# Graph-attention kernel: q and k taken from the fp16 halves of m, cosines of unnormalised m with the threshold subtracted in PSUM, and cross-partition maxima by TensorE

## The reference, cut to what matters

```python
# layer 0: 8 heads of 64, h = relu(layernorm(x)), 128 x 128 x 512
m   = h @ map_w.T + map_b
n   = m_head / max(norm(m_head), 1e-8)
adj = (n @ n.T > 0.1)                       # cosine threshold, per head
q   = m @ q_w.T + q_b ;  k = m @ k_w.T + k_b
p   = softmax(mask(q @ k.T / 8)) * keep
a   = adj * p
v   = h @ gcn_map_w.T + gcn_map_b
x   = x + relu((a @ v) @ gcn_W.T / (a.sum(-1) + 1))
# layer 1: 4 heads of 64, plain masked attention
h1  = relu(layernorm(x));  x = x + attention(h1 @ Wq, h1 @ Wk, h1 @ Wv, mask) @ Wo + bo
```

## Time and profile before

| what | value |
|---|---|
| median of 3 runs | 2621.02 us (2617.14 to 2621.39) |
| profiled execution | 2623.38 us, its span 2621.6 us |
| mean granted TensorE clock | 0.989 of full speed |
| PE busy | 2554.7 us, 97% of the span |
| PEld busy | 2056.4 us, 78% |
| POOL busy | 2164.7 us, 83% |
| DVE busy | 2068.1 us, 79% |
| ACT busy | 1709.5 us, 65% |
| DMA | 299 MB moved, engines busy 61% of the time in the steady part |

### The profile page before, as it was taken

How to read it: one execution, slowest core, us unless ns; L and a number is a source line. 1 busy time by engine, 2 the same in 40 slices (tenths; PEclk the granted TensorE clock), 3 DMA queues, 4 the chain that set the end, 5 groups by cost and what they waited for, 6 DMA issues and landing times.

```text
span 2621.6 us, 78827 instructions
## 1 busy us (share of the span) xinstructions
PE 2554.7 (97%) x30681; PEld 2056.4 (78%) x30681; DVE 2068.1 (79%) x3467; ACT 1709.5 (65%) x4509; POOL 2164.7 (83%) x2450
## 2 busy tenths in 40 slices
PE   6899999999999999999999999999999999999995
PEld 4678878887887887887887887887888888788784
DVE  6478788788888888788878888888888888888875
ACT  3366676676676676676676667667667667667664
POOL 2388888888888888888888888888888888888874
PEclk8999999999999999999999999999999999999998
DMA  5145665665665665665665666566566556556554
GB/s 134 45 83 115 121 119 112 121 123 108 118 129 102 118 129 103 120 125 113 115 125 111 117 121 117 111 125 117 112 121 124 113 113 129 112 112 129 109 95 97
DMA packets 830707, 299.08 MB, mean 114 GB/s; under 512 B 772608, under 2 KB 780288, under 8 KB 830336
## 3 DMA queue, kind: packets, MB, share of 16 engines
q1 hardware_dynamic: 830336, 294.04, 57.9%
HBM read 75.80 MB, written 33.55 MB: 42 GB/s over the span
## 4 chain that ended last, share of the span: by engine, by line
PE 90%; DVE 3%; POOL 2%; issue 2%; DMA 2%; ACT 1%; SPq 0%; DVEq 0%; ACTq 0%; POOLq 0%
PE unit_ps L1563 49%; PE unit_ps L1571 24%; PE s_ps L1581 4%; PE s_ps L1623 3%; PE c_ps L1581 3%; PE unit_ps L1642 2%; PE unit_ps L1657 2%; PE unit_ps L1581 2%; PE unit_ps L1633 1%; DMA o_t<-o_hl 1%; DVE qk_hl L1131 1%; POOL inv_norm L700 1%; ACT e_ec L828 0%; ACT qk_hl L918 0%; PE c_ps L1520 0%
## 5 line engine op out<-in xcount | busy, mean ns | idle before, releaser
L828 ACT ACTIVATE e_ec<-e_ec,neg_mx 128x128 f32<-128x128 f32 x1016 | 392.9, 388 | 4.1
L1563 PE MATMUL unit_ps<-h_t,w_m_hi 128*128 128x256 f16 x2048 | 343.1, 275 | 12.6 <-DMA h_t<-h_hl 12.6
L1563 PE MATMUL unit_ps<-h_t,w_q_hi 128*128 128x256 f16 x2048 | 345.0, 274 | 2.6 <-DVE bias_q L1382 2.6
L1563 PE MATMUL unit_ps<-h_t,w_k_hi 128*128 128x256 f16 x2048 | 345.3, 274 | 0.1
L1571 PE MATMUL unit_ps<-w_v_hi,h_t 128*128 128x512 f16 x1024 | 324.9, 379 | 0.0
L651 POOL TENSOR_TENSOR e_ec<-e_ec 128x1024 f16<-128x1024 f32 x126 | 285.9, 2269 | 12.1 <-ACT e_ec L856 12.1
L1563 PE MATMUL unit_ps<-h_t,w_m_lo 128*128 128x256 f16 x1024 | 280.8, 274 | 0.0
L1563 PE MATMUL unit_ps<-h_t,w_k_lo 128*128 128x256 f16 x1024 | 280.5, 274 | 0.0
L1563 PE MATMUL unit_ps<-h_t,w_q_lo 128*128 128x256 f16 x1024 | 280.1, 274 | 0.0
L1131 DVE TENSOR_TENSOR qk_hl<-qk_sb,qk_hl 128x512 f16<-128x512 f32 x128 | 173.2, 1353 | 121.0 <-ACT qk_hl L918 121.0
L1563 PEld LDWEIGHTS unit_ps<-h_t,w_m_hi 128*128 128x128 f16 x2048 | 196.4, 98 | 42.4 <-issue 13.1
(11 more groups left out here) (207 smaller groups left out, 7736.7 us busy)
## 6 DMA issues: line engine op xcount, KB each, us to landing
xa<-in_x_dram SPq DMA_DIRECT2D x128, 256.0 KB, 3.7
xres<-in_x_dram SPq DMA_DIRECT2D x128, 256.0 KB, 2.8
out_dram<-ybuf SPq DMA_DIRECT2D x128, 256.0 KB, 2.5
h_t<-h_hl SPq DMA_TRANSPOSE x256, 3.2
ec_t<-e_ec SPq DMA_TRANSPOSE x254, 3.2
adj_in<-in_adj_dram SPq DMA_DIRECT2D x128, 16.0 KB, 2.0
p_t<-p_hl SPq DMA_TRANSPOSE x128, 3.3
o_t<-o_hl SPq DMA_TRANSPOSE x128, 3.7
```

Source lines behind the costliest of these rows:

```text
L828: ins = nc.scalar.activation(e[:, h, :], e[:, h, :], ACT.Exp, bias=neg[:, h:h + 1], scale=SCALE, accum_out=sums[:, h:h + 1])
L1563: ins = nc.tensor.matmul(out, w[a][:, i, c * P:(c + 1) * P], h[:, :, b, i, :], start=n == 0, stop=n == len(passes) - 1)
```

## The change

q and k are now made from `m`: its two fp16 halves (`m_hl`, double buffered, made by ScalarE `m_upper` and GpSimd `m_lower` in the even slot, right after `m`) are the moving operand of `q` and `k`, and the weights `q_w` and `k_w` are only turned and split. The same halves are both operands of the cosines, without any division: into the same PSUM bank TensorE adds a product that is -0.1 \* |m_i| \* |m_j| (`norm_t`, `norm_r`), and `gate` compares with 0. The norms (power +1/2) are cut into fp16 parts by GpSimd, turned by two small matmuls (unit `nt`), and VectorE's `threshold_rows` writes them out as `norm_t` (128x128) and `norm_r` (128x1024, times a mask of -1). Maxima over partitions come from a transpose, a VectorE maximum and a small matmul; for six weights the sum of squares takes the place of the maximum. SP loads `x` first. `m_upper` stands in ScalarE's even slot between `e_upper` and the second `l1_exp`. In the prologue `make` and `bias` go, for q and for k. The split of layer 1's weights moves from the prologue into slots 0 and 1. One of the two `result_base` goes from the even to the odd slot.

```diff
 UNITS = (
     (("s1a", -4), ("s1b", -4), ("m01", 2), ("m23", 2), ("wo", -5), ("va", 2), ("lv", -4), ("vb", 3)),
-    (("q01", 1), ("o1e", -5), ("q23", 1), ("o1o", -4), ("norm", 1), ("k01", 1), ("lq", -3), ("bc0", 1), ("bc1", 1), ("k23", 1),
+    (("q01", 1), ("o1e", -5), ("q23", 1), ("o1o", -4), ("norm", 1), ("k01", 1), ("lq", -3), ("k23", 1), ("nt", 1), ("unused", B_MAX),
      ("lk", -3), ("wo", -5)),
 )
...
+            load_x(Slot(-5, None, B))
             load_columns(st_map, map_w, map_in)
-            load_x(Slot(-5, None, B))
-            load_weights()
-            for n in (-3, -2, -1):
+            load_first_weights()
+            first = Slot(-3, None, B)
+            turn_x(first)
+            load_adj(first)
+            load_x(first)
+            load_other_weights()
+            for n in (-2, -1):
...
-            def inverse_norms(s):
+            def norm_rows(s):
-                    nc.gpsimd.tensor_tensor(inv_norm[:, :], sq_sum[:, :], minus_half[:, :], ALU.pow).then_inc(inv_norm_done, 1)
+                    nc.gpsimd.tensor_tensor(norm[:, :], sq_sum[:, :], plus_half[:, :], ALU.pow).then_inc(norm_done, 1)
...
+                    nc.gpsimd.tensor_copy(parts[:, :, 1:4, :], rows.unsqueeze(2).broadcast_to([P, 2, 3, 2 * C])).then_inc(norm_split, 1)
+                    nc.gpsimd.tensor_tensor(parts[:, :, 0:5:4, :], rows.unsqueeze(2).broadcast_to([P, 2, 2, 2 * C]),
...
-            def directions_lower(s, g):
-                    nc.gpsimd.tensor_tensor(dir_hl[:, 1, :, cols], m_sb[:, :, cols], dir_hl[:, 0, :, cols],
-                                            ALU.subtract).then_inc(dir_lo, 1)
+            def m_lower(s):
+                if s.has(2):
+                    b = (s.n + 2) // 2 % 2
+                    pool.wait_ge(m_hi, s.at(lambda t: (t + 2) // 2 + 1))
+                    nc.gpsimd.tensor_tensor(m_hl[:, b, 1], m_sb[:, :, :], m_hl[:, b, 0], ALU.subtract).then_inc(m_lo, 1)
...
+            def m_upper(s):
+                    nc.scalar.activation(m_hl[:, b, 0], m_sb[:, :, :], ACT.Copy).then_inc(m_hi, 1)
...
-            def directions(s, g):
+            def threshold_rows(s):
+                    nc.vector.tensor_copy(norm_t[:, :], unit_ps[:, u.bank, 0:P])
+                    nc.vector.tensor_tensor(norm_r[:, :, :, :].rearrange("p g c n -> p (g c) n"),
...
             def cosines(s):
-                    row_pairs([[c_ps[:, a, c * P:(c + 1) * P] for c in range(C)] for a in range(2)], dir_hl, dir_hl,
-                              columns(s.n % 2)).then_inc(c_full, 1)
+                    row_pairs([[c_ps[:, a, c * P:(c + 1) * P] for c in range(C)] for a in range(2)], parts, parts,
+                              columns(s.n % 2), last=False)
+                    u = s.unit("nt", back=1 + s.n % 2)
+                    pe.wait_ge(unit_out[u.bank], u.before + 1)
+                    for a in range(2):
+                        r = slice(a * DK, (a + 1) * DK)
+                        ins = nc.tensor.matmul(c_ps[:, a, :], norm_t[r, :], norm_r[r, s.n % 2].rearrange("p c n -> p (c n)"),
+                                               start=False, stop=True)
...
-            make("make_q", "turn_q")
-            bias("bias_q")
-            evicted("make_q")
+            evicted("turn_q")
             qk_part(before_0, "q", w_q, 0)
```

More of the change, by code:

```diff
@@ L41 @@
 UNROLL = 8
[L45 to L48, removed]
+NAMED = 14
+MAP, MAP_B, GM, QW, KW, L_FIRST = 0, 4, 5, 8, 9, 10
+M, M_OUT, V, V_OUT, Q, K, LQ, LK, WO, LV, LV_OUT = range(11)
+SCALED = 11
 BLOCKED = 1e30
@@ L421, in build @@
-        ONES = 4
-        def prep_at(kind, part=0):
-            u = PREP.index((kind, part))
-            place = u - C
-            if place < 0:
-                return unit_ps[:, part], None, 0, u + 1
-            bank = (s_ps[:, place % 4].rearrange("p b n -> p (b n)") if place % 4 < 2 else c_ps[:, place % 4 - 2])
-            return bank, prep_out[place % PREP_BANKS], place // PREP_BANKS, u + 1
+                (p1_sb[:, :, :, :].rearrange("p b h n -> p (b h n)").rearrange("p (c n) -> p c n", c=C), Wv, w_lv, LV)]
@@ new lines, in build @@
+        ONES = 14
+        def prep_at(kind, part=0):
+            full = PREP.index((kind, part)) + 1
+            if kind == "turn_m":
+                return unit_ps[:, part], None, 0, full
+            if kind in SMALL:
+                return s_ps[:, 0].rearrange("p b n -> p (b n)"), prep_out[0], SMALL.index(kind), full
+            place = STAGED.index(kind) * C + part
+            bank = (s_ps[:, 1].rearrange("p b n -> p (b n)"), c_ps[:, 0], c_ps[:, 1])[place % 3]
+            return bank, prep_out[1 + place % 3], place // 3, full
@@ L1581, in row_pairs @@
                             ins = nc.tensor.matmul(outs[half][c], st[r, a, c, cols], mv[r, b, c, cols],
-                                                   start=n == 0, stop=n == 2)
+                                                   start=n == 0 and (last or c == 0), stop=last and n == 2)
                 return ins
@@ L1673, in qk_part @@
                 if s.has(1):
-                    features(s, f"{name}{2 * half}{2 * half + 1}", w, 2 * half, h_t[:, (s.n + 1) // 2 % 2])
+                    pe.wait_ge(m_lo, s.at(lambda t: (t + 1) // 2 + 1))
+                    ps = start_unit(s, f"{name}{2 * half}{2 * half + 1}")
+                    parts = m_hl[:, (s.n + 1) // 2 % 2]
+                    for c in (2 * half, 2 * half + 1):
+                        passes = [(i, a, b) for b in range(2) for i in range(C) for a in range(2 - b)]
+                        for n, (i, a, b) in enumerate(passes):
+                            ins = nc.tensor.matmul(ps[:, c % 2 * 2 * P:(c % 2 + 1) * 2 * P], w[a][:, i, c * P:(c + 1) * P],
+                                                   parts[:, b, i, :], start=n == 0, stop=n == len(passes) - 1)
+                    ins.then_inc(unit_full, 1)
             def v_part(s, name, a):
```

500 lines of the change are left out of this document (280 added, 220 removed).

## The result

The changed kernel takes 2659.55 us (median of 4 runs, 2658.73 to 2663.12), the kernel before on the same chip 2621.2 (2617.14 to 2626.93). The ratio is 1.0147 with a 95% interval of 1.0126 to 1.0169: slower by 38 us, where 2662 was forecast.

A forecast was written before the change was run, and what follows sets the result against it. PE was taken to bound the steady part, with a new wait at lk after the change. 2623.4 - 36 (prologue) + 77 (pairs) = 2664, or 2662 us for the median; range 2635 to 2700 (58%), 8 in 10 within 2560 to 2715.

The forecast's parts named there:

- The prologue's term: Before slot 0: -38.6 us, plus 2.6 for layer 1's weights in slots 0 and 1, sum -36; slot 0 near 64.
- the pairs': Steady part: a pair of 40.2 us against 38.92, +1.28 each, +77 us for 60 pairs.
- The bound before: Steady part before the change: as long as PE's work, busy 2313.55 of 2320 us, with POOL next.
- PE's own sum: PE's work in a steady pair: -0.87 + 0.11 + 0.43 = -0.33 us, so 38.45 if PE stays the bound.
- The place and the mechanism: Before lk in the odd slot: later x_lower and k_lower held by POOL's e_lower make PE wait 1.75 us.
- The second of the two ways: Start of lk by POOL's queue order: e_lower ends 17.0 to 17.7 us into the odd slot, lk at 18.2 to 18.9.
- the one late pair of before: Trace pair with x_lower 5.71 us into the odd slot and lk at 18.78; model for the 18.7 taken.
- the 1.10 us of room: Before lk: lqk_lower frees the bank at about 363.57, PE comes at 364.67; this room hid POOL's work.
- rival A: Steady part: the chain to lk keeps off PE, a pair is 38.45 us, the kernel 2557 to 2570; chance 20%.
- The cause of the late landing: POOL's even slot: m_lower, 2.13 us behind e_lower, delays x_lower and behind it SP's o_hl transpose.
- 0.15 us taken: VectorE's odd slot: threshold_rows stands ahead of the next mask and adds 0.15 us to a pair's chain, between 0 and 0.65.
- rival D: Steady part: PE's clock falls in the new pause, costing up to 240 us, or 20 to 60; 13% shared with another rival.

The follow-up runs named there:

- e12: e10 with GpSimd's two small operations of keep_and_block moved, in odd slots, from ahead of x_lower to just ahead of e_lower; 2563.17 us.
- e3: The changed kernel without the 128x1024 instruction of threshold_rows from slot 0 on; 2656.39 us.
- e4: The changed kernel with m_lower on VectorE, behind x1_stats of the even slot, in place of GpSimd; 2651.79 us.
- e5: The changed kernel with SP's transposing DMA of o_hl issued ahead of the two loads of x in the odd slot; 2581.45 us.
- e8: The changed kernel with four moves in the prologue's order on ScalarE and VectorE, steady part as it is; 2647.23 us.
- e9: The changed kernel without GpSimd's m_lower from slot 1 on; 2630.79 us.
- e10: The changed kernel with the moves of e5 and e8 together; 2573.38 us.
- e1: The kernel before with one more GpSimd subtraction of 128x1024 behind e_lower in each even slot, its result unread; 2736.98 us.

## Why the prediction was right, and where it was not

The sum of the changes by stage, from the two traces: until slot 6, 190.88 - 213.55 = -22.7 us; the 59 pairs to slot 124, (2541.17 - 190.88) - (2510.01 - 213.55) = +53.8; the end, 117.1 against 111.6, +5.5. Together +36.7, the difference of the spans (2658.3 - 2621.6). The prediction had -36 and +77. The prologue's term was too large by 13 us, the pairs' by 23, the end (+5.5) was not in it; the errors cancelled, and that 2662 is so near to 2659.55 is luck; the parts don't deserve it.

The bound before, and PE's own sum: right. 38.45 for PE's pair was met to the hundredth in the won pairs and in e12. The two 512-column cosine matmuls cost 0.22 a slot (17.50 against 17.28).

The place and the mechanism: right in what was seen, too coarse in what decides. `lk` waits in 55 of 59 pairs, for `lqk_lower` behind `k_lower`, which the lock holds until POOL's `e_lower` is over. The second of the two ways (by POOL's order) gave `e_lower`'s end as 17.0 to 17.7 and `lk` as 18.2 to 18.9; measured 17.00 and 18.35. `x_lower` began 5.59 us into the odd slot, not 6.0 to 6.5, which is why `e_lower`'s end is at the near end. I took 18.7, from the one late pair of before, and these 0.35 us are the whole error of the forecast pair (40.2 against 39.87 in a usual one). The direct reading of the queue was better than the nearest disturbed pair, which had its own delay.

What I did not see is that this is a race and not a sum. Seven kernels have the changed steady part with `e_lower` mostly at 14.87 us into the slot (the changed one, e3, e4, e5, e8, e9, e10); they have 413 pairs from slot 6 to slot 124. In 129 `k_lower` starts 0.01 us or more ahead of `e_lower`: each is won and takes 38.45 us (two at slot 6 take 38.65 and 38.68). The other 284 are late, at 39.84 us or more; in two of them the records have `k_lower` ahead by less than 0.01. Where `e_lower` starts later the border moves with it. In the kernel before (mostly 15.22) and in e1 (mostly 16.05 or 16.37), 118 more pairs, all with a lead of 0.04 us or more are won and all others wait at `lk`; so it is the order that decides and not a time in the slot. The page "SBUF — State Buffer" of the Trainium skill (section "SBUF: two separate sides") says that whichever of the two operations starts first has the shared ports for its whole length; the prediction used the exclusion but not the "first". These pairs agree with it. In the kernel before `e_lower` starts at 15.22 and `k_lower` at 14.43 in the median: 53 of 59 pairs are won. In the changed kernel it is 14.87 and 15.86: 3 of 59.

So the 1.10 us of room in the prediction was not used up in proportion: lateness costs nothing as long as `k_lower` starts first, and a hair more costs 39.86 - 38.45 = 1.41 us. It costs no more than that until `k_lower` comes behind `e_lower`'s end at 17.00, which one pair did. The condition that I wrote for rival A, that `o_hl` could land 1.7 us earlier, is what e5 brought about: in the median it is issued at 9.51 instead of 11.16 us into the slot, and `k_lower` starts at 14.09. A was one moved line away.

The cause of the late landing: half right. `m_lower`, the only thing that I put ahead of `x_lower`, is 0.87 of 1.67 us [e9]. I had priced `m_upper` on ScalarE at nothing, because its own reader doesn't wait; what is queued behind it, the second p half, makes POOL wait 0.70. A further 0.35 us of the lost lead have nothing to do with the landing: `e_lower` starts earlier than before (14.87, not 15.22), because two copies of 1.17 together became two of 0.22 and 0.24. POOL had less work there, and that helped the wrong party.

`threshold_rows`: 0.15 us taken, 0.01 measured in a late pair [e3]. That the mask would be late was wrong; it starts 0.95 behind the scores as before.

The clock (rival D): one pair after slot 6 had it. The rival's rows had a slow stretch after a pause of 2.23 us and none after 1.12. There `o_hl` landed at 16.46 into the slot and PE paused 2.47 us:

```profile
427.25 0.40 PE L1646 MATMUL unit_ps<-h_t,w_lk_hi 128*128 128x256 f16 x2 [2.47 <-DVE lq_hl L1199]
...
427.65 0.64 PE L1646 MATMUL unit_ps<-h_t,w_lk_hi 128*128 128x256 f16 x2
...
428.29 0.64 PE L1646 MATMUL unit_ps<-h_t,w_lk_hi 128*128 128x256 f16 x2
```

The matmuls of `lk` then ran at half rate (0.64 us from one such row to the next, 0.33 in the pairs without it): from 428 to 432 us the granted clock was 0.64 in the mean, where it was 1.00 from 420 to 427, so it had fallen to the lower of its two levels (1.2 GHz) for most of that stretch. The pair took 42.74. The usual pause of 1.25 never did that.

The prologue: -26.6 us at slot 0, outside the forecast's own bounds of -28 to -46. m began at 21.78 (forecast 21). Behind that I added up PE's work and took the other engines' queues as ready. They weren't: PE stood 5.28 us at 41.25, 2.87 at 56.18, 1.31 at 60.78 and 2.41 at 66.71, each time for an instruction that was ready but behind another one. e8 took 6.3 us out of these four; slot 0 came 9.2 earlier, and the whole kernel was 12.3 faster.

Still open: why the time from the issue of `o_hl` to its landing varies so much (3.0 to 5.9 us in the changed kernel, 2.6 to 4.9 in e5, up to the start of ScalarE's `o1_upper`). Nothing was tried on it.

## What to carry to other kernels

Where two engines exclude each other, don't add up delays: find the two instructions that meet and ask which comes first, and by how much. A shift of a tenth cost 1.41 us here or nothing. The cheapest repair was to move a DMA issue (78 us) or two small operations so that the order is safe; removing the 2.13 us of work gave 29. But look at whom the moved instruction meets next: the same move made the kernel before slower. For an added instruction, price what stands behind it in its queue, on every engine that it touches.

## What the hardware showed

- When VectorE loses the meeting, its instruction ends 0.55 us after the winner's end (`k_lower`, 0.69 us alone, took up to 2.7), and the winner is not slowed: `e_lower` keeps its 2.13. When GpSimd loses by a hair, `e_lower` takes 2.57 to 2.67, only 0.5 more.
- Small operations suffer as well: a 128x2 GpSimd operation took 1.17 instead of 0.23 us beside a 1.21 us subtraction on VectorE [e4].
- A VectorE operation with one input in PSUM was not held by GpSimd's: `lqk_lower` took 0.74 to 0.75 us in every pair, beside `e_lower` as well as beside `result_base`.
- The issue of the two 256 KB loads of x keeps SP for 0.8 to 2.3 us (1.06 in the median), and whether it stands ahead of `o_hl`'s or behind it decided between 2581 and 2660 us here.
